# Making wo's high and low parts in the first passes of the layer stage instead of in the first stage

## The reference

```
# token stage: a diagonal state-space kernel of length 1024 for each token
Wc = Wc * num * reciprocal(den * Lam)
K  = einsum('chn,hnl->chl', Wc, exp(dt_Lambda * pos))        # h = K.real, (64, 128, 1024)
# one transformer layer
h = h + attn(layernorm(h), Wq, Wk, Wv, Wo)   # 32 heads of 32, 8 key/value heads, rope, causal; ctx @ Wo
h = h + ffn(layernorm(h), A, B, Wr, br)      # 8 routed low-rank experts of rank 16
```

## Time and profile before

| what | before |
|---|---|
| median of 3 runs | 2432.23 us |
| the profiled execution | 2433.67 us |
| its span, first to last instruction | 2431.9 us |
| mean granted PE clock | 0.983 |
| PE busy | 2298.0 us (94%) |
| DVE busy | 1984.0 us (82%) |
| ACT busy | 1828.7 us (75%) |
| POOL busy | 1709.9 us (70%) |

### The profile page before, as it was taken

How to read it: one execution, slowest core, us unless ns; L and a number is a source line. 1 busy time by engine, 2 the same in 40 slices (tenths; PEclk the granted TensorE clock), 3 DMA queues, 4 the chain that set the end, 5 groups by cost and what they waited for, 6 DMA issues and landing times.

```text
span 2431.9 us, 58560 instructions
## 1 busy us (share of the span) xinstructions
PE 2298.0 (94%) x18704; PEld 1249.2 (51%) x18704; DVE 1984.0 (82%) x7796; ACT 1828.7 (75%) x6270; POOL 1709.9 (70%) x1529
## 2 busy tenths in 40 slices
PE   2998489999999999999999999999999999999986
PEld 2777244555555555555555555555555555555543
DVE  8999468888888888888888888888888888888864
ACT  5988277777777787777777777777777777777773
POOL 1444087777777777777777777787777777777771
PEclk9999799999999999999999999999999999999997
DMA  2887389999999999999999999999999999999984
GB/s 67 265 252 241 109 150 177 185 186 187 185 190 181 191 187 184 184 190 190 185 183 189 185 183 189 188 186 184 190 186 185 186 190 188 179 193 181 185 163 98
DMA packets 1199524, 443.63 MB, mean 182 GB/s; under 512 B 1149552, under 2 KB 1151856, under 8 KB 1199216
## 3 DMA queue, kind: packets, MB, share of 16 engines
q1 hardware_dynamic: 1199216, 439.89, 91.3%
HBM read 87.42 MB, written 67.11 MB: 64 GB/s over the span
## 4 chain that ended last, share of the span: by engine, by line
PE 71%; ACT 6%; DVE 5%; DMA 3%; issue 2%; POOL 1%; SPq 1%; POOLq 0%; ACTq 0%; DVEq 0%
PE pb L852 8%; PE pa L852 8%; PE pb L853 8%; PE pb L854 8%; PE pa L854 7%; PE pa L853 7%; PE s_ps L866 4%; PE pc L852 4%; PE pc L853 4%; PE pc L854 4%; ACT pr L1004 4%; PE pv_ps L881 3%; PE pd L852 1%; DMA pt<-p 1%; PE pd L854 1%
## 5 line engine op out<-in xcount | busy, mean ns | idle before, releaser
L1004 ACT ACTIVATE pr<-pr,smin 128x128 f32<-128x128 f32 x2048 | 792.6, 388 | 191.1 <-DVE smin L1145 191.1
L1350 POOL TENSOR_TENSOR pr<-pr,rinv 128x512 f32<-128x512 f32 x512 | 576.9, 1137 | 355.8 <-DVE rinv L1153 345.2
L1358 POOL TENSOR_TENSOR p<-pr,p 128x512 f16<-128x512 f32 x512 | 590.1, 1158 | 117.8 <-ACT p L1014 111.3
L1145 DVE CUSTOM_DVE_ANT_0 pr<-s_ps,cst 128x128 f32<-128x128 f32 x2048 | 471.5, 286 | 150.3 <-POOL p L1358 107.2
L1014 ACT ACTIVATE p<-pr 128x512 f16<-128x512 f32 x512 | 319.0, 623 | 170.7 <-POOL pr L1350 150.9
L1004 ACT ACTIVATION_READ_ACCUMULATOR pr<-pr,smin 128x1 f32 x2048 | 382.2, 187 | 0.0
L611 PE MATMUL hps<-z,xw 128*128 128x256 f32 x848 | 194.7, 390 | 62.9 <-POOL xw L321 42.0
L852 PE MATMUL pa<-wkv_hi,xt 128*128 128x512 f16 x512 | 194.9, 381 | 28.5 <-DMA xt<-xs 28.5
L611 PEld LDWEIGHTS hps<-z,xw 128*128 128x128 f32 x848 | 163.5, 195 | 93.7 <-POOL xw L321 50.1
L866 PE MATMUL s_ps<-kt,qt 128*128 128x128 f16 x2048 | 199.1, 220 | 8.9 <-DVE smin L1145 5.0
L866 PEld LDWEIGHTS s_ps<-kt,qt 128*128 128x128 f16 x2048 | 149.5, 98 | 106.8 <-DVE smin L1145 5.8
(11 more groups left out here) (192 smaller groups left out, 5561.1 us busy)
## 6 DMA issues: line engine op xcount, KB each, us to landing
h<-hout SPq DMA_DIRECT2D x128, 256.0 KB, 3.8
h_ln<-h SPq DMA_DIRECT2D x64, 512.0 KB, 4.2
h_res<-h SPq DMA_DIRECT2D x64, 512.0 KB, 4.5
out<-h SPq DMA_DIRECT2D x64, 512.0 KB, 3.2
pt<-p SPq DMA_TRANSPOSE x512, 3.9
xa<-x SPq DMA_DIRECT2D x16, 256.0 KB, 4.1
xb<-x SPq DMA_DIRECT2D x32, 128.0 KB, 3.8
wst<-wq SPq DMA_DIRECT2D x8, 512.0 KB, 6.0
```

The lines of the kernel that those rows point to most:

```text
L1004: last = A.activation(p, p, ACT.Exp, bias=smin[g % 2][:, j:j + 1], scale=-1.0, accum_out=rsum[g % 2][:, j:j + 1])
L1145: V.tensor_tensor_reduce(pr[g % 2][:, cols], s_ps[g % 2][:, cols], mask, 1.0, 3e38, ALU.add, ALU.min, smin[g % 2][:, j:j + 1]).then_inc(ma ...
L1350: nc.gpsimd.tensor_tensor(p3, p3, rinv[g % 2][:, :].unsqueeze(2).broadcast_to([P, HG, P]), ALU.mult).then_inc(p_norm, 1)
L1358: nc.gpsimd.tensor_tensor(p[:, HG * P:], pr[g % 2][:, :], p[:, 0:HG * P], ALU.subtract).then_inc(pl_done, 1)
```

## The change

`wo` is taken out of the first stage: `PIECES` has no `wo` any more, and `aw` and `bm` move to windows 2 and 6, where `wo`'s first two pieces stood. In the layer stage the 8 pieces of `wo` are loaded into five buffers that the first bodies don't use yet (`wo_at`), ACT's `weight_high` and DVE's `weight_low` make the parts, and both are placed between the bodies: on DVE and ACT the first five pieces between body -2 and body -1, the last three between body -1 and body 0; on SP the first five loads between body -3 and body -2, the last three between body -2 and body -1. The last three reuse the first three buffers, so SP waits for `wo_lo` before each. The last hunk is DVE's; ACT's is the same with `weight_high`.

```diff
-            PIECES += [(4 * k + 1, "wq", k, D, 1), (4 * k + 2, "wo", k, D, 1), (4 * k + 3, "wkv", k, 512, 2)]
+            PIECES.append((4 * k + 1, "wq", k, D, 1))
             if k < 2:
-                PIECES.append((4 * k + 4, ("aw", "bm")[k], None, (KC * AW, D)[k], 1))
+                PIECES.append((4 * k + 2, ("aw", "bm")[k], None, (KC * AW, D)[k], 1))
+            PIECES.append((4 * k + 3, "wkv", k, 512, 2))
...
+        wo_at = (h2, h1[0], h1[1], xn, h_res)
...
+                def load_wo(k):
+                    n = k % len(wo_at)
+                    if k >= len(wo_at):
+                        sp.wait_ge(wo_lo, n + 1)
+                    sp.dma_start(wo_at[n][:, :], wo[k * P:k * P + P, :]).then_inc(wo_in[n], 16)
...
                 def load_res(b):
+                    if b == 0:
+                        sp.wait_ge(wo_lo, KC)
...
-                bodies(sp, body)
+                body(-3, 1)
+                for k in range(len(wo_at)):
+                    load_wo(k)
+                body(-2, 0)
+                for k in range(len(wo_at), KC):
+                    load_wo(k)
+                for i in range(-1, NB + 3):
+                    body(i, i % 2)
...
                 def wo_half(b, odd, half, k0, k1):
+                    if k0 == 0 and b == 0:
+                        pe.wait_ge(wo_lo, KC)
...
                 def norm_apply(w, b, odd):
+                    if w and b == 0:
+                        act.wait_ge(wo_lo, KC)
...
+                def weight_high(k):
+                    act.wait_ge(wo_in[k % len(wo_at)], 16 * (k // len(wo_at) + 1))
+                    A.activation(W["wo_hi"][:, k, :], wo_at[k % len(wo_at)][:, :], ACT.Copy, scale=WS).then_inc(wo_hi, 1)
...
+                def weight_low(k):
+                    dve.wait_ge(wo_hi, k + 1)
+                    V.scalar_tensor_tensor(W["wo_lo"][:, k, :], wo_at[k % len(wo_at)][:, :], WS, W["wo_hi"][:, k, :],
+                                           ALU.mult, ALU.subtract).then_inc(wo_lo, 1)
...
-                bodies(dve, body)
+                body(-3, 1)
+                body(-2, 0)
+                for k in range(len(wo_at)):
+                    weight_low(k)
+                body(-1, 1)
+                for k in range(len(wo_at), KC):
+                    weight_low(k)
+                for i in range(NB + 3):
+                    body(i, i % 2)
```

More of the change, by code:

```diff
@@ L121, in vit_layer, with s4_stage @@
         }
-        s4_stage(nc, x, log_dt, lam, wq, wk, wv, wo, aw, bm, br, consts, h0, W)
-        layer_stage(nc, h0, out, W)
+        s4_stage(nc, x, log_dt, lam, wq, wk, wv, aw, bm, br, consts, h0, W)
+        layer_stage(nc, wo, h0, out, W)
 V_F, V_X, V_E, V_T, N_PRE = 15, 16, 17, 26, 49
-def s4_stage(nc, x, log_dt, lam, wq, wk, wv, wo, aw, bm, br, consts, h0, W):
+def s4_stage(nc, x, log_dt, lam, wq, wk, wv, aw, bm, br, consts, h0, W):
     with ExitStack() as ctx:
@@ L233, in s4_stage @@
         for k in range(CHUNKS):
-            PIECES += [(4 * k + 1, "wq", k, D, 1), (4 * k + 2, "wo", k, D, 1), (4 * k + 3, "wkv", k, 512, 2)]
+            PIECES.append((4 * k + 1, "wq", k, D, 1))
             if k < 2:
-                PIECES.append((4 * k + 4, ("aw", "bm")[k], None, (KC * AW, D)[k], 1))
-        SRC = {"wq": (wq,), "wo": (wo,), "wkv": (wk, wv), "aw": (aw,), "bm": (bm,)}
+                PIECES.append((4 * k + 2, ("aw", "bm")[k], None, (KC * AW, D)[k], 1))
+            PIECES.append((4 * k + 3, "wkv", k, 512, 2))
+        SRC = {"wq": (wq,), "wkv": (wk, wv), "aw": (aw,), "bm": (bm,)}
         def loads_until(n):
@@ L615, in _, with layer_stage @@
                             last.then_inc(tok_done, 1)
-def layer_stage(nc, h0, out, W):
+def layer_stage(nc, wo, h0, out, W):
     with ExitStack() as ctx:
@@ L675, in layer_stage @@
         h2 = sb("h2", [P, D])
+        wo_at = (h2, h1[0], h1[1], xn, h_res)
         s_ps = [ps(f"s_ps{i}") for i in range(2)]
         pv_ps, pa, pb, pc, pd, tx = (ps(n) for n in ("pv_ps", "pa", "pb", "pc", "pd", "tx"))
+        wo_in = [sem(f"wo_in{i}") for i in range(len(wo_at))]
+        wo_hi = sem("wo_hi")
+        wo_lo = sem("wo_lo")
         ln_in = sem("ln_in")
@@ L1130, in _ @@
                 A.preload_act_table_set("natural_log_exp_and_others")
-                bodies(act, body)
+                body(-3, 1)
+                body(-2, 0)
+                for k in range(len(wo_at)):
+                    weight_high(k)
+                body(-1, 1)
+                for k in range(len(wo_at), KC):
+                    weight_high(k)
+                for i in range(NB + 3):
+                    body(i, i % 2)
             @block.vector
```

## The result

The changed kernel takes 2440.75 us (median of 8 runs, 2436.71 to 2444.47) beside 2431.36 us of the kernel before (8 runs): ratio 1.004, 95% interval 1.0031 to 1.0050, so 9.4 us slower. A second set of runs gave 1.0034 (1.0022 to 1.0047). I had forecast 5.8 us slower. The time lies inside my range of 2433 to 2443, but 9.4 lies beyond the 7.3 us up to which I called it "same", the case to which I had given 0.61. The profiled execution has a span of 2442.7 us, 10.8 more than before.

A forecast was written before the change was run, and what follows sets the result against it. PE bounds from 331 us on; before that, three nearly full engines in the first stage, then a chain of waits. Costs 0.7 + 6.8 + 0.8 + 6.0 = 14.3, gain 8.5: 5.8 us slower, 2438.0 us from the median, range 2433 to 2443.

The forecast's parts named there:

- same: Whole kernel: time within 0.3%, 7.3 us, of the kernel before, 2424.9 to 2439.5; chance 0.61.
- First place: Layer stage, DVE: five low parts between the halves of x_low of sequence 1, with POOL's lock, cost 6.8 us.
- the sum: Whole kernel: predicted costs 14.3 us less gain 8.5 us, so 5.8 us slower.
- the gain of the first stage: First stage without wo: PE's gaps shrink as DVE comes sooner, 8.5 us gained, bounds 2.2 to 11.5.
- PE can use the two gaps behind it: First stage, chunks without a wo piece: PE closes gaps of 0.29 and 1.11, 1.40 us in all.
- rival 1: First stage: ACT or the stores keep the period, only 2.2 us gained, 12.1 slower, 2444.3 us; chance 0.18.
- the second place: Layer stage, ACT and DVE: last three high and low parts delay the chain to sequence 2 by 6.0 us.
- PE's clock: Layer stage, sequence 1: longer PE idle time prolongs the lower clock level, costing 0.8 us, at most 1.3.
- the first loads: Start of layer stage: five wo loads behind the first h_ln load cost 0.7 us, bounds 0 to 2.6.
- rule on ring order: Start of layer stage: descriptors taken in ring order, so first h_ln loses nothing and the loads' term would be 0.2.
- Rival 2: Layer stage: low parts hide in DVE's idle time, 7.8 us faster, 2424.4 us; chance 0.09.
- Rival 3: First stage: all PE gaps close, gain 11.5 us, so 2.8 slower, 2435.0 us; chance 0.09.

The follow-up runs named there:

- early loads: Loads of x, from the fourth on, issued one window earlier in the first stage: changed kernel 2431.93 us (1.0014 to before); kernel before, same edit, 0.9996.
- The experiment gives 6.2 to 6.8: Changed kernel with only the last three high parts moved right behind x_high and low parts right behind x_low of sequence 1: 2428.87 us.
- The fastest kernel of the study: Changed kernel with all low parts and the last three high parts moved into idle time, and loads of x one window earlier: 2418.74 us, 0.9953 to before.
- the loads issued late: Changed kernel with all eight loads of wo behind the transposed transfer of sequence 0 on the queue: 2437.90 us.
- 16.0 in the experiment: Kernel before, still making wo's parts in its first stage, with the changed kernel's layer stage making them again: 2444.68 us, 16.0 more.

## Why the prediction was right and wrong

**Right: the direction and the mechanism.** The low parts in front of a step of the chain cost what they last. First place: 6.76 us from xt 0 to xt 1 against 6.8 in the sum, 6.7 over all traces, and 7.1 came back when only they moved. (That the one trace agrees to 0.04 us is luck: the second gave 5.5.) POOL's share of it is seen too. Three low parts took 5.52 us with POOL's `qr` and `qs` beside them, 4.57 where `qs` had moved away, 3.50 with POOL idle. The changed kernel, DVE and then POOL:

```profile
290.60 5.52 DVE L1230 SCALAR_TENSOR_TENSOR wo_lo<-h,wo_hi 128x1024 f16<-128x1024 f32 x3
```

```profile
290.17 1.65 POOL L1416 TENSOR_TENSOR qr<-rt_c,rt_s 128x512 f32<-128x512 f32 x1 [0.77 <-DVE rt_s L1250]
292.56 1.35 POOL L1423 TENSOR_TENSOR qs<-qr,qs 128x512 f16<-128x512 f32 x1 [0.74 <-ACT qs L1082]
```

I had added 1.1 for one POOL instruction. In the trace the whole excess over 3.50 is 2.0, but 1.1 of it is what `x_low` had lost before, so the term came out near the truth. The Trainium skill (SBUF — State Buffer, Who interferes with whom) says that a VectorE instruction with two SBUF inputs contends with a GpSimd instruction that reads SBUF; the trace agrees, with 5.52 us for 3.50.

**Mis-sized: the gain of the first stage, 8.5 in the sum, 6.3 measured (6.1 over seven traces).** This is the larger error. From the changed trace, against the earlier trace rows, by stretches from chunk start to chunk start (chunks counted from 0; the rows' titles call the one from 126.11 chunk 4, it is number 3): chunks 2 and 3 gave 2 x 26.64 less 50.56 (98.61 to 149.17), 2.7, as said (2.8). Chunk 4 gave 0.55 for 1.40; chunk 5, 1.97 for 2.1; chunk 6, 1.22 for 2.2; chunk 7 lost 1.27; chunks 0 and 1 gave 0.86 where I had nothing. The step that failed is "PE can use the two gaps behind it": it treats ACT as having room, since it loses 1.0 us of work per chunk. But SP's loads of `x` are issued by the windows' own progress and ACT then meets them too early: 12.9 us of wait for 5.7. That is my rival 1's mechanism at part strength. It took some 5 us of an 11.8 us gain, not all, so the rival's number, 2444.3, didn't come. The bounds held (2.2 to 11.5), and the upper one is about what the stage gives with early loads (11.8). That I had 8.5 and not 11 is partly a second error: each closed gap also saved 0.24 us of PE's busy time (24.88 us per chunk in three records, 24.41 in one), which I had not counted. (6.3 counts to SP's first `h_ln` load; the stretches above add to 6.05, up to the last matmul.)

**Mis-sized: the second place, 6.0 in the sum.** PE's first matmul on sequence 1 to that on sequence 2 grew by 7.7 us (27.93, 35.64). Of it 1.05 us are the clock's (below) and 6.7 the place's. DVE's wait for `x_high` was 2.11 us, where I had 2.7, and the three low parts took 4.01 instead of 3.4, as the upper bound had it. The experiment gives 6.2 to 6.8 for the place, and all traces together 6.5.

**Missed: the second transposed transfer.** From the issue of xt 1 to PE's first matmul, 5.28 us before, 6.61 in the changed kernel. It took 6.3 to 6.5 in the other traces in which the last three loads of `wo` were issued 5 to 7 us ahead of it, and 5.1 to 5.4 in those where they left earlier or weren't there. The fastest kernel of the study is between, 5.77. The sum had nothing there, only that the waiting loads "hold up only the load of row 2".

**Near the trace only by chance: PE's clock, 0.8 in the sum, 1.05 in the trace.** I took the lower level to last longer after a longer idle time. These are the last record at 0.6 us and the first at 0.4 us in the changed kernel, 5.5 us behind 306.01:

```profile
311.11 0.61 PE L870 MATMUL pb<-wq_hi,xt 128*128 128x512 f16 x1
311.53 0.40 PE L871 MATMUL pb<-wq_lo,xt 128*128 128x512 f16 x1
```

The same stretch in all twelve traces: after 11 to 12 us of idle PE (the changed kernel's two among them) 5.5, 5.0, 5.0, 5.8, 5.8 and 2.8 us; after 4 to 4.6 us (the kernel before first) 3.6, 3.4, 3.3, 5.5, 5.9 and 2.8. The two groups overlap. Their means, 5.0 and 4.1 us, differ by 0.9 us at half speed, so by a cost of 0.4 to 0.5 us, and the scatter in any one trace is some 1.5 us of the level to either side, so 0.8 of cost. These traces don't show that the term is a cost of the change.

**Not shown: the first loads, 0.7 in the sum.** See the loads issued late. Nor can these runs tell the 0.7 from the 0.2 of the rule on ring order in the Trainium skill (DMA: Bandwidth & Descriptors, Queues, rings and completion order).

Rival 2 (hidden in idle time) was wrong for this order, and right for another one: with both sets of parts a few instructions earlier all of it is hidden. Rival 3 (all gaps close) didn't come here either; with the loads of `x` issued earlier it did.

In sum: costs 14.3 in the sum, 16.65 in the first trace and 16.0 in the experiment (12.9 to 19.0); gain 8.5, 6.3 and 4.9. By the first trace alone both sides seem wrong, by 2.2 and 2.4 us. The other traces say otherwise. From SP's first `h_ln` load to PE's first matmul on sequence 2 the five kernels with both places in the path took 81.6 to 84.7 us (mean 82.5), the three without `wo` in the layer stage 65.9 to 69.0 (mean 67.7). That is a cost of 14.8 us, against a gain of 6.1: together 8.7 us, between the 8.3 and 9.4 that were measured. So the costs were right within 0.5 us, in part because the missed second transfer, 1.1 us, stood against loads and clock that cost less than their terms or nothing. The error of 3.6 us comes mostly from the gain, 2.4 us too high, and it carried the time over the bound of "same".

## What to carry to other kernels

Work moved into idle time must be put where the engine's queue waits, not where its average is low: here a shift by a few instructions turned 9 us slower into 6 us faster. When one engine's load on a shared bound is cut, ask what the next one waits for before counting all gaps as gain; a wait for loads that was small and harmless, 5.7 us, grew to 12.9 and took nearly half of the gain. Read a mark such as the start of one transfer in several traces before giving meaning to less than 1.5 us of it.

## What the hardware showed that I had not expected

- PE's lower clock level after an idle time lasted from 2.8 to 5.9 us in the same place of twelve traces: 2.8 to 5.8 after 11 to 12 us of idle PE, 2.8 to 5.9 after 4 to 4.6.
- A transposed transfer that took 5.1 to 5.4 us, from its issue to PE's first matmul, took 6.3 to 6.6 with three 512 KB loads issued 5 to 7 us ahead of it.
- Three low parts on DVE (128x1024, float32, two inputs) took 3.50 us with POOL idle, 4.57 with one of its additions beside them and 5.52 with two.
- The load of the first row, 512 KB, took 3.7 to 6.3 us where five more of the same size were issued right behind it, and 3.2 to 4.9 us where none was: the two ranges overlap.
